# Attention setup by batch in a two-layer transformer kernel, with a late modulation and a folded value bias

## The reference, cut to what matters

```python
q_lat = hidden_states @ Wq_down.T + bq_down          # hidden_states: normed, modulated x
kv_lat = hidden_states @ Wkv_down.T + bkv_down
q_half = q_lat @ Wq_up.T + bq_up
q = concatenate([q_half, rotary(q_half)], -1)        # k in the same way from kv_lat
v = kv_lat @ Wv_up.T + bv_up                         # 16 heads of 16
attn = softmax(q @ k.T / 4)                          # per head, 512 x 512
out = (attn @ v) @ Wo.T + bo
```

## Time and profile before

| what | value |
|---|---|
| median of 3 runs | 838.84 us (838.81 to 839.66) |
| the profiled execution's own time | 838.84 us |
| its span, first to last instruction | 836.7 us |
| PE busy | 766.1 us, 92% |
| first score tile | 33.78 us |
| first step of the loop | 71.79 us |
| fourth group (g = 3) starts | 109.46 us |
| last values matmuls of the attention start | 163.44 us |

### The profile page before, as it was taken

The page is one execution under the profiler, slowest core; times in us unless marked ns, Lnnn a source line. Parts: engine busy times, 40 slices in busy tenths (PEclk is TensorE's granted clock), DMA queues, the critical chain, the costliest instruction groups (busy, mean ns, idle before and its releaser), DMA issues. The chain is left out here.

```text
span 836.7 us, 11472 instructions
## 1 busy us (share of the span) xinstructions
PE 766.1 (92%) x3972; PEld 566.3 (68%) x3983; DVE 541.6 (65%) x1320; ACT 259.3 (31%) x411; POOL 206.6 (25%) x190
## 2 busy tenths in 40 slices
PE   5899999999999999999899599898885899999995
PEld 4323333358788888888545388777752799999995
DVE  4566998366655455455689999999578353334345
ACT  2222776735334444343464212022230100000000
POOL 2420000003223232221003000678000344344421
PEclk9895999998999999999999889999998999999997
DMA  8564300010111111113031503500012899999973
GB/s 293 168 184 99 62 3 4 2 57 20 38 56 49 45 56 38 56 38 133 1 113 51 213 1 99 129 2 0 2 51 94 312 348 345 339 347 342 340 261 102
DMA packets 38574, 102.36 MB, mean 122 GB/s; under 512 B 5296, under 2 KB 16944, under 8 KB 38128
## 3 DMA queue, kind: packets, MB, share of 16 engines
q1 hardware_dynamic: 34640, 92.32, 33.9%
q0 software_dynamic: 3632, 9.05, 2.9%
q10 hardware_dynamic: 256, 0.39, 0.3%
HBM read 84.25 MB, written 17.56 MB: 122 GB/s over the span
## 5 line engine op out<-in xcount | busy, mean ns | idle before, releaser
L1369 PE MATMUL psum<-xr,wr 128*128 128x512 f32 x600 | 146.3, 394 | 1.0 <-DVE arena L2018 1.0
L1369 PEld LDWEIGHTS psum<-xr,wr 128*128 128x128 f32 x600 | 114.2, 191 | 25.6 <-issue 1.7
L755 POOL TENSOR_TENSOR wr<-ring,wr 128x512 fp32r<-128x512 f32 (+1 forms) x50 | 55.0, 1117 | 261.3 <-ACT wr L918 147.5
L1863 DVE TENSOR_REDUCE small<-psum 128x1 f32<-128x512 f32 x128 | 81.5, 685 | 24.8 <-PE psum L1249 24.4
L1684 PEld LDWEIGHTS psum<-arena 128*128 128x128 f32 x700 | 83.5, 192 | 3.4 <-issue 1.7
L1684 PE MATMUL psum<-arena 128*128 128x128 f32 x700 | 84.0, 275 | 1.1 <-ACT arena L1122 1.1
L1694 PE MATMUL psum<-arena 128*128 128x256 f32 x350 | 81.3, 379 | 0.0
L2481 DVE TENSOR_SCALAR arena<-psum,arena 128x256 f32<-128x256 f32 x35 | 16.9, 484 | 93.6 <-PE psum L1694 93.6
L1380 PE MATMUL psum<-hr,wr 128*128 128x512 f32 x300 | 76.6, 391 | 0.9 <-DVE hr L1955 0.9
L893 ACT ACTIVATE arena<-psum 128x1024 f32<-128x1024 f32 x64 | 62.5, 1026 | 38.5 <-PE psum L1258 38.3
L1981 DVE TENSOR_TENSOR hid<-hid,psum 128x512 f32<-128x512 f32 x50 | 34.4, 688 | 60.2 <-ACT hid L924 60.0
(11 more groups left out here) (383 smaller groups left out, 1211.7 us busy)
## 6 DMA issues: line engine op xcount, KB each, us to landing
arena<-in_w1u SPq DMA_DIRECT2D x35, 642.5 KB, 5.8
arena<-in_w1d SPq DMA_DIRECT2D x35, 640.0 KB, 5.2
ring<-in_w SPq DMA_DIRECT2D x25, 384.0 KB, 3.0
z_scratch<-w_a SPq DMA_DIRECT2D x4, 768.0 KB, 7.1
arena<-z_scratch SPq DMA_DIRECT2D x8, 384.0 KB, 6.6
part_scratch<-arena SPq DMA_DIRECT2D x8, 256.0 KB, 3.9
part_scratch<-arena SPq DMA_DIRECT2D x4, 512.0 KB, 2.7
qkv_scratch<-arena SPq DMA_DIRECT2D x4, 512.0 KB, 2.6
```

Source lines behind the costliest of these rows:

```text
L755: pool.tensor_tensor(wr0[:, k, LO, part], ring0[:, k, part], wr0[:, k, HI, part], ALU.subtract).then_inc(s["w0_lo"], 1)
L1369: ins = pe.matmul(bank[2 * b + m][:, :], wr0[:, k, w, lo:lo + P], xr[:, x, f, half(b)], start=(f == 0 and (w, x) == PARTS[0]), stop=(f == ...
L1863: dve.tensor_reduce(own[:, at:at + 1], full("scores", n), AX, ALU.max, negate=True).then_inc(s["bank_free"], 1)
```

## The change

- The groups go batch by batch: b = g // 4, t = g % 4. Latent, up-projection, values, parts and rows are made for batch 0 first. All rows tiles are per batch and group, so that rows come in 8 sets of 8 DMAs, each of 512 tokens.
- The start loads x in two halves with a semaphore each; `ccol` and the first modulation weights are issued by ACT.
- The run-up has 26 score tiles. Batch 1's up-projections and values stand among its first 9; spare matmuls only from tile 10 on.
- The 2.5 MB of modulation weights are loaded after the maxima of group 2 and the rows of the last group, into space freed by batch 1's parts. The 5 wide products stand in the loop at group 4, step 1, their transposes at group 4, step 4.
- The maxima of group g+1 come at step p = 4 (the lookahead is 26), the last ones at (6, 4).
- The value bias is no longer added to the values: `Wo` times the bias is made once (8 small matmuls at group 4, step 4) and added to the output bias. ACT copies the values out of PSUM where DVE did.
- The three PSUM slots have a full and a free semaphore each.

```diff
-FIRST = HG * TB + 12
+FIRST = HG * TB + 10
@@ SP's order
-            parts_out(0, 0, half(0))
-            ...
-            for g in range(NG):
-                ... maxima of g ...
-                if g < 2:
-                    all_rows(2 + g)
-                    ones_rows(sp, 2 + g, f"ones_in{2 + g}")
+            parts_out(0, 0)
+            parts_there(0, 0)
+            k_rows(sp, 0, 0)
+            both_rows(0, 1)
+            parts_out(0, 1)
+            load("ld_rows", rows[:, :], a["rows"])
+            parts_there(0, 1)
+            both_rows(0, 2)
+            maxima_in(0)
+            both_rows(0, 3)
+            parts_out(1, 0)
+            load("ld_g", w_g[:, :, :], a["w_g"])
+            load("ld_g", consts[:, :], a["consts"])
+            parts_there(1, 0)
+            both_rows(1, 0)
+            maxima_in(1)
+            parts_out(1, 1)
+            both_rows(1, 1)
+            parts_there(1, 1)
+            both_rows(1, 2)
+            maxima_in(2)
+            both_rows(1, 3)
+            for t in (2, 3):
+                ones_rows(sp, 1, t, "ones_late")
+            load("ld_mod1", wmod[0], a["wmod"][0, :, :, 2 * D:])
+            load("ld_mod1", wmod[1], a["wmod"][1])
+            for g in range(3, NG):
+                maxima_in(g)
@@ TensorE, start
+            latent(0)
+            pe.wait_ge(s["lat_in"], 1)
+            for t in UP_ORDER:
+                up(0, t)
+            latent(1)
+            for m in range(2):
+                values_in(m)
@@ TensorE, run-up
             for n in range(FIRST):
                 scores_and_maxima(n)
-                if n == 3:
-                    pe.wait_ge(s["ld_mod1"], 32)
-                    pe.wait_ge(s["v_in"], NT // 2)
-                if n in range(3, 3 + 2 * MODC, 2):
-                    modulate_rows((n - 3) // 2)
-                elif n == 3 + 2 * MODC + 2:
-                    mod_turned()
-                else:
-                    warm(1, 5 if n < 3 else 2)
+                if 1 <= n <= 4:
+                    if n == 4:
+                        pe.wait_ge(s["v_in"], 2)
+                    up(1, UP_ORDER[n - 1])
+                if n in (6, 8):
+                    if n == 8:
+                        high_made(pe, 1, 0, 0)
+                    values_in(2 + (n - 6) // 2)
+                if n >= 10:
+                    if n == 10:
+                        pe.wait_ge(s["up_copy"], 3)
+                        pe.wait_ge(s["ld_sel0"], 32)
+                    warm(1, 6)
@@ TensorE, loop
+                    if (g, p) == MOD_DUE:          # (4, 1)
+                        mod_in_rows()
+                    if (g, p) == MOD_TURN_DUE:     # (4, 4)
+                        mod_turned()
```

More of the change, by code:

```diff
@@ L534, in slot, with full_sem, free_sem, uses @@
             return SLOTS[bank_turn[name] % len(SLOTS)]
+        def full_sem(name):
+            return s[f"full{slot(name)}"]
+        def free_sem(name):
+            return s[f"free{slot(name)}"]
+        def uses(name):
+            return bank_turn[name] // len(SLOTS) + 1
         def head_rows(x, jb, r, end):
             return x[jb * HROW + r:jb * HROW + end]
-        def piece_rows(n, t, r, end, jb):
+        def piece_rows(n, b, t, r, end, jb):
             part = (QP, KP)[n][r]
             rows = part_dram[n, t // 2, part:part + end - r].rearrange("x (d t j o) n -> (x d) t o j n", t=2, j=HP, o=2)
-            return rows[:, t % 2, jb]
@@ L545, in rows_in, with high_made, low_made @@
-        def rows_in(t, b):
-            return f"ld_rows_{t}" if t else f"ld_rows_0{b}"
-        def k_rows(eng, t, own, name):
+            return rows[:, t % 2, jb][:, :, half(b)]
+        def rows_in(b, t):
+            return f"ld_rows_{b}{t}"
+        def high_made(eng, b, pair, n):
+            eng.wait_ge(s["hi"], 4 * b + 2 * pair + n + 1)
+        def low_made(eng, b, pair, n):
+            if (b, pair) == (0, 0):
+                eng.wait_ge(s["lo_dve"], n + 1)
+            else:
+                eng.wait_ge(s["lo_pool"], 4 * b + 2 * pair - 2 + n + 1)
@@ L580, in _, with parts_out @@
-            load("ld_mod1", wmod[1], a["wmod"][1])
-            load("ld_g", consts[:, :], a["consts"])
-            def parts_out(pair, before, own):
+            def parts_out(b, pair):
                 for part in (HI, LO):
                     for n in range(2):
-                        sp.wait_ge(s[f"part{part + 1}"], before + n + 1)
-                        load(f"parts_out{pair}", part_dram[n, pair, part][:, own],
-                             (high[:, 2 * n + pair], low[2 * n + pair])[part][:, own])
@@ L604, in _, with parts_there, both_rows @@
-            parts_out(1, 2 * B, slice(0, TOK))
-            for g in range(NG):
-                sp.wait_ge(s["bank_free"], bank_turn["maxima", g] + 1)
+                        (high_made, low_made)[part](sp, b, pair, n)
+                        load("parts_out", part_dram[n, pair, part][:, half(b)], piece(b, n, pair, part))
+            def parts_there(b, pair):
+                sp.wait_ge(s["parts_out"], 16 * 4 * (2 * b + pair + 1))
+            def both_rows(b, t):
+                k_rows(sp, b, t)
+                q_rows(sp, b, t)
@@ L858, in _, with up_out, high_turned @@
             norm_out(0)
-            for b in range(B):
+            def up_out(b, t, to):
+                act.wait_ge(s["up"], 4 * b + UP_ORDER.index(t) + 1)
+                return act.activation(to, bank[UP_BANKS[b][t]][:, :], ACT.Identity, bias=cols[:, BUP + t:BUP + t + 1])
+            def high_turned(b):
                 for n in range(2):
-                    act.wait_ge(s["up"], 2 * b + n + 1)
-                    act.activation(high[:, 2 * n, half(b)].bitcast(F32R), bank[4 * b + 2 * n][:, :], ACT.Identity,
-                                   bias=cols[:, BUP + 2 * n:BUP + 2 * n + 1]).then_inc(s["part1"], 1)
@@ L865, in _ @@
[L865 to L869, removed]
-                if b == 0:
-                    act.wait_ge(s["parts_out0"], 16 * 4)
-                    q_rows(act, 0, half(0), rows_in(0, 0))
-            act.wait_ge(s["mod_mm"], 2)
@@ L874, in _ @@
[L874 to L878 removed]
+                    act.wait_ge(s["rotated"], 2 * b + n + 1)
+                    act.activation(piece(b, n, 1, HI).bitcast(F32R), turned_rows[b][n], ACT.Copy)\
+                       .then_inc(s["hi"], 1)
@@ new lines, in values_out @@
+            def values_out(m):
+                act.wait_ge(s["v_mm"], m + 1)
+                act.activation(V[:, 2 * m:2 * m + 2, :, 0:HD],
+                               bank[V_BANKS[m]].rearrange("p (t h d) -> p t h d", t=2, h=NH), ACT.Copy)\
+                   .then_inc(s["v_in"], 1)
+            for n in range(2):
+                up_out(0, 2 * n, piece(0, n, 0, HI).bitcast(F32R)).then_inc(s["hi"], 1)
+            act.wait_ge(s["parts_out"], 16 * 4)
+            q_rows(act, 0, 0)
+            for m in range(2):
+                values_out(m)
@@ new lines, in _, with mod_rows_out @@
+            high_turned(0)
+            for n in range(2):
+                up_out(1, 2 * n, X1[:, 2 * n]).then_inc(s["up_copy"], 1)
+                up_out(1, 2 * n, piece(1, n, 0, HI).bitcast(F32R)).then_inc(s["hi"], 1)
+            for n in range(2):
+                up_out(1, 2 * n + 1, X1[:, 2 * n + 1]).then_inc(s["up_copy"], 1)
+            for m in range(2, NT // 2):
+                values_out(m)
+            def mod_rows_out():
+                for x in range(2):
+                    name = "mod_rows", x
+                    act.wait_ge(full_sem(name), uses(name))
+                    act.activation(mod_rows[:, x, :], bank[slot(name)][:, :], ACT.Copy).then_inc(free_sem(name), 1)
@@ L1236, in next_bank @@
+                    ins.then_inc(full_sem(("mod", x)), 1)
+                to = next_bank("out_bias")
+                for m in range(KD):
+                    for k in range(KD):
+                        ins = pe.matmul(to[:, m:m + 1], wo[:, k, tile(m)], cols[:, BV + k:BV + k + 1],
+                                        start=(k == 0), stop=(k == KD - 1))
+                ins.then_inc(full_sem(("out_bias",)), 1)
             def next_bank(*name):
-                if bank_turn[name] >= len(SLOTS):
-                    pe.wait_ge(s["bank_free"], bank_turn[name] - len(SLOTS) + 1)
+                if uses(name) > 1:
+                    pe.wait_ge(free_sem(name), uses(name) - 1)
@@ L1849, in mod_in @@
+            for n in range(2):
+                up_times(2 * n + 1, sw[:, n, half(0)], 1)
+            latent(1)
             def mod_in():
-                dve.wait_ge(s["mod_mm"], 3)
+                to = full("mod", 0)
                 dve.tensor_copy(mod_all[:, first:first + 16 * B].rearrange("p (c n b) -> p n c b", c=4, b=B),
-                                bank[4].rearrange("p (n c x) -> p n c x", n=4, x=Q)[:, :, :, 0:B])
+                                to.rearrange("p (n c x) -> p n c x", n=4, x=Q)[:, :, :, 0:B])\
+                   .then_inc(free_sem(("mod", 0)), 1)
```

(1 more changed line is left out.)

348 lines of the change are left out of this document (186 added, 162 removed).

## The result

The changed kernel takes 850.18 us (median of 4 runs, 846.1 to 854.58); the kernel before, on the same chip, takes 838.83 us (4 runs, 838.13 to 839.66). The ratio is 1.0136, with a 95% interval of 1.0084 to 1.0188: slower, by some 11 us. The profiled execution of the changed kernel is one of 854.58 us (span 852.3), so the traces differ by 15.74 us, 4.4 more than the medians.

What follows compares the result with a forecast made beforehand. TensorE's chain of waits was taken as the bound, with room in the run-up. From 838.84, 5.4 gained up to group 3, 11.4 for modulation and 0.8 for the last maxima gave 845.6 us; own range 841 to 850, wide range 832 to 852.

Steps and rivals of the forecast that it cites:

- the clock stays low: Rival, chance 0.17: tiles 10 to 25 of the run-up at half clock, the loop 5 us later, 850.6 us.
- The prediction's own sign: Check in the profile after: if the run-up takes over 30 us, the clock decided.
- Start: Up to the first score: rows requested 1.4 us earlier, their way 5.7 instead of 7.0 us; gain 2.6 us.
- Run-up: First score to loop: loop starts at 57.9, not 71.79, 11.3 us gained beyond the start; group 0 gains 3.6.
- The forecast's own upper bound: Run-up all at half clock: ten tiles at 0.5 us each, 5 us more.
- SP's queue: Maxima landing behind rows, parts and weights: TensorE waits 6.0, 2.3 and 3.8 us at groups 1 to 3, 12.1 lost.
- The other estimate: SP's queue by the skill page: rows take 1.8 us of data, three waits lose some 2 us each, near 840.
- Modulation: Wide products, transposes and bias products in group 4, hidden by nothing: 20 records at 0.43 us and more, cost 11.4 us.
- Last maxima: Last group's maxima, sent one step later, 1.3 us, where before they were just in time: cost 0.8 us.
- The queue keeps up: Rival, chance 0.33: maxima 1 to 3 come before TensorE needs them, the 12.1 us goes, 833.5 us.

Runs made afterwards that it cites:

- Experiment 1: Changed kernel with 30 spare matmuls between batch 0's values and the first score tile: 840.07 us, 1.0019 of the kernel before.
- experiment 2: Experiment 1 plus one spare matmul ahead of each of score tiles 5 to 9: 842.72 us, 1.0051 of the kernel before.
- 9: experiment 6 with a second spare matmul in every other run-up tile from tile 10 on: 831.5 us, 0.9902 of the kernel before.
- experiment 6: experiment 5 with 28 instead of 26 run-up tiles and the last maxima at step 3: 831.88 us, 0.9912 of the kernel before.
- experiment 5: Changed kernel with the spare matmuls of experiment 2 and the SP order of experiment 3: 834.16 us, 0.9943 of the kernel before.
- experiment 3: Changed kernel, SP's order alone: maxima ahead of rows, modulation weights behind maxima 3, modulation in group 5: 845.72 us, 1.0065 of the kernel before.
- Experiment 8: experiment 6 with the wide products in the loop made twice: 837.78 us, 0.9967 of the kernel before.
- 4: Kernel before with its five wide products in a row at tile 3 instead of between tiles: 829.54 us, 0.9895 of the kernel before.
- 12: Kernel before, wide products in a row, spare matmuls ahead of the first score, extra ones between run-up tiles and in group 0: 825.46 us, 0.9843.
- 11: Kernel before with 9 spare matmuls ahead of its first score tile, nothing else: 839.38 us, ratio 1.0.
- 7: Kernel before with wide products in a row and 9 spare matmuls ahead of the first score: 830.3 us, 0.9878 of the kernel before.

## Why the prediction was right or wrong, point by point

The time came out at 850.18, in the range of 832 to 852 and slower as forecast, but just outside the forecast's own 841 to 850. It is nearly the time of the rival "the clock stays low" (850.6), and the sum reached its 845.6 by errors that cancel. The prediction's own sign said so: a run-up of over 30 us means that the clock decided, and it took 36.8.

*Start: right in size, by luck.* Gain 2.9 where 2.6 was forecast; first score at 30.88 (31.2). But the two terms were 1.4 from an earlier request of the rows and 1.2 from their shorter way. The request came 3.3 earlier (23.50 against 26.81) and the way took 7.4 us, not 5.7 (that it "may stay 7.0" was the prediction's own doubt):

```profile
23.50 1.73 SPq L606 DMA_DIRECT2D k_rows<-part_scratch  x4
```

So TensorE, done at 24.5 and not "near 26 or 27", had the longer to wait.

*Run-up: this is the step that failed.* I wrote "TensorE … is then idle for some 4 us, so the clock will be low; I take it low for the first two up-projections". It was idle for 6.37 us and stayed at half clock for all 36.8 us of the run-up and all of group 0, from 28.4 to 83.0: run-up and group 0 gave 1.2 − 1.5 = −0.3 instead of 11.3 + 3.6. The forecast's own upper bound for a run-up all at half clock, 5 us more (26.7 + 5 = 31.7), was still 5 too short, since it charged only ten tiles. Experiment 1 shows the cause: filled, the run-up takes 25.3 us and the kernel 10.1 less. What I had not asked is what brings the clock back. Before, it rose at 41.9, behind the first wide product (37.29 to 40.86; the second stands in the earlier trace rows), and these products had been moved away. That they lifted it is not shown, and the trace after speaks against it: from 31.60 to 48.0 TensorE is reported busy without a gap there, with eight records of 128x512 from the up-projections (two stand at 39.78) and eight of the values among the tiles, and the clock did not rise. What was shown is that spare matmuls ahead of the tiles (1) and between them (2, 9) keep it up for a time. The Trainium skill's page "TensorE: Matmul & The Clock Gate", section "HAM oscillation — how this bites in real kernels", says that a wait for data throws the array back to its slow clock; in its example the waits take some 3 to 5 us. The falls behind the waits at 96.62 and 166.80 agree with it, and here waits of 1.6 and 2.6 were enough (the groups behind them grew by 5.0 and 3.1 us); the fall at 45.7 in experiment 6 has no wait at all, so keeping TensorE from waiting is not enough.

*SP's queue: right in kind, its first wait too large.* Forecast 6.0, 2.3 and 3.8 us. In the trace after, groups 1, 2 and 3 wait 0, 1.6 and 0.2: with TensorE at half clock the maxima had time. Once the run-up is fast, they are 0.8, 3.4 and 2.9 (experiment 2), 7.1 in all against 12.1, and the order is worth 8.6 us (5 against 2), about 4.5 where the run-up is slow (3, intervals that overlap). The timetable itself held there: counted from the end of group 0's copy (51.2), the maxima of groups 1, 2 and 3 were used at 20.6, 36.0 and 53.0, where 20.7, 34.9 and 50.6 were forecast. SP reached the first two 2.0 and 2.1 us after they were copied; the rest of their delay is landing. The third it reached at once, as they were copied only at 45.7, so that their agreement is partly chance. What the forecast had wrong is when TensorE wants them: group 0 ran at 0.55 of the clock and took 15.1 us, not 10.3, so group 1's wait was 0.8 and not 6.0. What it would be with group 0 at full clock was not run. The other estimate (waits of some 2 us, near 840) uses a figure that the Trainium skill's page "DMA: Bandwidth & Descriptors", section "Anatomy of one DMA — SWDGE (gpsimd) path", gives for DMAs issued by gpsimd, and SP issues these. The landings behind rows were 2.6 to 3.0 us, near the forecast 3; behind the modulation weights 3.5 to 4.4, not 7.

*Modulation: the mechanism right, the term mis-sized.* Nothing hid it, but group 4 grew by 4.9, and the work took 3.60 + 1.07 + 0.99 = 5.7 us against 11.4. I took 0.43 us a record from products that stood alone; in a row they take 0.18. Experiment 8 measured it by itself: 3.4 us for twenty more. In the code, the first four products write to different 32-row strips of one bank and the fifth to another bank. The first four's part, as a stretch of the trace after with L1326 alone (PE, PEld, PEclk, DMA), and TensorE's timeline at its first 0.4 us:

```profile
128.74:130.46 1.72, 1.71 (x16) 0.43 (x16) 1.00 0.00 0
```

```profile
128.75 0.62 PE L1326 MATMUL psum<-arena,ccol 128*2 128x512 f32 x4
```

Four records start together, and the sixteen of four products pass in 1.72 us, four steps of 0.43, the time of one product; the fifth, alone, takes the remaining 1.88. So the step of 0.43 was right and the number of steps wrong: 8, not 20. The same page of the Trainium skill, section "Part 3: Packing small matmuls — row/col tiling", has such matmuls run side by side and gives 2.38 times for three column strips. The trace agrees that they do, and shows more: 4 times for four strips.

*Last maxima: mis-sized.* 0.8 forecast. The wait was 2.57, since max_scratch landed after 2.9 us instead of the 1.4 or so that it needs alone, and the low clock behind it cost 3.1 more. One profiled run can't say how often that is so; in the trace before, such landings go up to 3.5.

*Rivals.* "The queue keeps up" would have given 833.5; experiment 5, which makes it nearly keep up and the run-up fast, measured 834.16, though with a low stretch in group 0 that the rival did not have. "The clock stays low" came true beyond its terms: all tiles, not 10 to 25. The values through ACT and the bias through the output have no measurement of their own; groups 1 and 3 less their waits (13.55 − 1.60 and 12.69 − 0.71, both 12.0 against 11.9) leave them no more than 0.1 us a group.

So of the 11.3 us between the medians, the clock of the run-up is 10.1 (1). The order of SP's queue costs 4.5 to 8.6, the modulation some 5, and the earlier first score gives 2.9 back. These don't add up, for the first two hide each other.

Open: what brings the clock back, and what decides where it falls among thin tiles. That the spread of the runs (14 us in experiment 3, 10.6 in 6, 1.8 in 4) comes from it is not shown.

## What to carry to other kernels

When a change leaves TensorE idle ahead of thin work, look at the granted clock behind the gap: here 6.37 us of idle time were followed by half clock through run-up and first group, and spare matmuls in the gap took 10.1 us off the kernel. If a stretch is late at half clock, look at what hides behind its lateness, here a DMA queue, before the waits in the same trace are believed. Small products into different strips of one bank belong in a row: this one edit to the kernel before (4) gained 9.3 us, 5.1 of it in the products themselves and most of the rest in the clock, and with spare matmuls beside it (12) 13.0.

## What the runs showed of the hardware that was not expected

- TensorE at half clock reports itself busy: 36.30 of 36.77 us in the run-up after. Only the granted clock and the 0.79 us of a score tile (0.50 at full clock) give it away.
- The clock falls among thin matmuls without a gap (6, at 45.7), and stayed low for 54.6 us in the kernel after, for 51.7 of which, run-up and group 0, TensorE is reported busy.
- Taking one low stretch away may only move the next and lengthen it: in 11 that from 35.1 to 41.9 went, and the one at 62.4 to 82.9 became 57.6 to 84.9; in 7 the same (65.9 to 72.7 became 46.1 to 73.4). The time didn't change in either.
- Twenty records of a 128x512 product with 2 output rows take 3.60 us in a row, 1.88 us for each four that stand alone. Four products into four strips of one bank pass in the time of one: 16 records in 1.72 us.
